# Extra edges in two lists of 64, one for each half of a pair, spread by products of 64 rows on two halves of the array

## What is computed

```python
summed = segment_sum(x[src], dst)
aggr = summed / max(count, 1)
h = aggr @ W_l.T + b_l + x @ W_r.T
h_norm = (h - mean(h)) * rsqrt(var(h) + 1e-5) * gamma + beta   # over the nodes
out = layernorm(x + relu(h_norm))                              # over the features
```

## Time and profile before

| | |
|---|---|
| median of 3 runs | 2502.92 us (2500.47 to 2504.99) |
| the profiled execution | 2496.8 us |
| its span, first to last instruction | 2495.1 us |
| mean granted TensorE clock | 0.853 |
| preparation and groups 0 to 7 | to about 172 us |
| loop over the pairs | first spread product 172.8 us, last 1736.2 us |
| second stage | behind about 1757 us |

### The profile page before, as it was taken

The page is one execution under the profiler, slowest core; times in us unless marked ns, Lnnn a source line. Parts: engine busy times, 40 slices in busy tenths (PEclk is TensorE's granted clock), DMA queues, the critical chain, the costliest instruction groups (busy, mean ns, idle before and its releaser), DMA issues. The chain is left out here.

```text
span 2495.1 us, 29831 instructions
## 1 busy us (share of the span) xinstructions
PE 1737.1 (70%) x9426; PEld 1411.9 (57%) x9426; DVE 1951.8 (78%) x3468; ACT 1471.2 (59%) x2847; POOL 1408.7 (56%) x688
## 2 busy tenths in 40 slices
PE   7999999999999999999999999998300000000000
PEld 5788888888888888888888888886100000000000
DVE  7846888888888888888888788887587777676666
ACT  4343555455554554555455545553499998888877
POOL 6034555555656655655556555556395655655654
PEclk9999999999999999999999999998755555555555
DMA  5567888878887888888888888888999999999998
GB/s 191 162 215 228 259 268 258 284 242 272 280 273 238 269 277 258 263 269 262 269 261 253 268 273 268 254 261 249 381 419 426 427 425 426 425 421 414 422 418 342
DMA packets 125536, 752.91 MB, mean 302 GB/s; under 512 B 20810, under 2 KB 20810, under 8 KB 65727
## 3 DMA queue, kind: packets, MB, share of 16 engines
q1 hardware_dynamic: 71710, 618.44, 65.9%
q0 software_dynamic: 53664, 132.51, 20.9%
HBM read 515.32 MB, written 246.22 MB: 305 GB/s over the span
## 5 line engine op out<-in xcount | busy, mean ns | idle before, releaser
L567 PE MATMUL pd<-wc_hi,x_hi 128*128 128x512 f32 x1564 | 626.7, 401 | 18.1 <-DVE wc_lo L970 15.3
L786 ACT ACTIVATE h_out<-pd 128x512 f32<-128x512 f32 x391 | 233.7, 598 | 656.8 <-PE pd L569 640.1
L569 PE MATMUL pd<-wc_hi,x_lo 128*128 128x512 f32 x1564 | 612.2, 391 | 0.0
L568 PE MATMUL pd<-wc_lo,x_hi 128*128 128x512 f32 x1564 | 609.3, 390 | 0.0
L1459 POOL TENSOR_TENSOR hx<-hx,scale_b 128x2560 f32<-128x2560 f32 (+2 forms) x99 | 441.3, 4478 | 286.1 <-DMA hx<-h_scratch 250.7
L1437 POOL DMA_INDIRECT h_scratch<-zz,si x156 | 324.2, 2078 | 412.1 <-ACT zz L832 192.9
L567 PEld LDWEIGHTS pd<-wc_hi,x_hi 128*128 128x128 f32 x1564 | 294.0, 188 | 75.5 <-issue 16.3
L930 ACT ACTIVATE hx<-hx,nr,rs 128x512 f32<-128x512 f32 x385 | 279.8, 802 | 89.0 <-DVE nr L1310 89.0
L569 PEld LDWEIGHTS pd<-wc_hi,x_lo 128*128 128x128 f32 x1564 | 293.7, 188 | 65.2
L568 PEld LDWEIGHTS pd<-wc_lo,x_hi 128*128 128x128 f32 x1564 | 294.6, 188 | 57.5
L1387 POOL DMA_INDIRECT xn<-x,gi x156 | 294.9, 1890 | 47.7 <-issue 44.3
(11 more groups left out here) (236 smaller groups left out, 3236.9 us busy)
## 6 DMA issues: line engine op xcount, KB each, us to landing
raw<-xT_whole SPq DMA_DIRECT2D x78, 1280.0 KB
h_scratch<-h_out SPq DMA_DIRECT2D x78, 1280.0 KB
hx<-x SPq DMA_DIRECT2D x78, 1280.0 KB, 20.6
hx<-h_scratch SPq DMA_DIRECT2D x77, 1280.0 KB, 15.4
out<-hx SPq DMA_DIRECT2D x77, 1280.0 KB, 18.1
hs<-h_scratch SPq DMA_DIRECT2D x76, 1280.0 KB
h_out<-h_scratch SPq DMA_DIRECT2D x2, 1280.0 KB, 7.3
xn<-x,gi POOLq DMA_INDIRECT x156
```

Source lines behind the costliest of these rows:

```text
L567: pe.matmul(pd[i][0:n, :], hi, wc["hi"][:, kc, :], start=kc == 0, stop=False)
L568: pe.matmul(pd[i][0:n, :], hi, wc["lo"][:, kc, :], start=False, stop=False)
L569: last = pe.matmul(pd[i][0:n, :], lo, wc["hi"][:, kc, :], start=False, stop=kc == KC - 1)
L786: act.activation(h_out[0:n, b, t, :], pd[(b + t) % 2][0:n, :], ACT.Copy).then_inc(s_ev, 1)
```

## The change

- The extras of half 0 are numbered 1 to 64 and those of half 1 from 65 to 128. For this DVE splits `member` by half (`b2["slot"]` for half 0, `vd` for half 1), sums those of half 0 over each window (`first_x`), and TensorE adds these over the partitions with one more bf16 product of 78 columns. DVE then subtracts this number from those of half 1 and adds 64. The bound for `left_over` is 64 for each half.
- The product of a half takes the 64 partitions of its list alone, so that there are four products with 64 rows, all ahead of the first plain tile, with the halves in turn. They increment `s_e` once, and the waits for it are changed to that.

```diff
+XH = P // 2
...
+        first_x = s0("first_x", [P, U], BF16)
...
-                last.then_inc(s_xrank, 1)
+                pe.matmul(p6[0:EB, 0:U], ones_b[0:EB, 0:EB], first_x[0:EB, :], start=True, stop=True).then_inc(s_xrank, 1)
...
-            def spread_extras(u, h):
-                if h == 0:
-                    pe.wait_ge(s_xel, u + 1)
-                    pe.wait_ge(s_spread, u + 1)
+            def spread_extras(u):
+
+                pe.wait_ge(s_xel, u + 1)
+                pe.wait_ge(s_spread, u + 1)
                 if u > 0:
-                    pe.wait_ge(s_d, 2 * u + h - 1)
-                to = spread[:, h * P:(h + 1) * P]
-                pe.matmul(spread_to[h][:], to, xe_hi[:], start=True, stop=False)
-                pe.matmul(spread_to[h][:], to, xe_lo[:], start=False, stop=True).then_inc(s_e, 1)
+                    pe.wait_ge(s_d, 2 * u)
+                for part in (xe_hi, xe_lo):
+                    for h in range(2):
+                        rows = slice(h * XH, (h + 1) * XH)
+                        last = pe.matmul(spread_to[h][:], spread[rows, h * P:(h + 1) * P], part[rows, :],
+                                         start=part is xe_hi, stop=part is xe_lo)
+                last.then_inc(s_e, 1)
...
                     if a is not None:
-                        spread_extras(a, 0)
+                        spread_extras(a)
                     plain(0)
-                    if a is not None:
-                        spread_extras(a, 1)
                     plain(1)
...
-                    act.wait_ge(s_e, 2 * u)
+                    act.wait_ge(s_e, u)
...
+            dve.scalar_tensor_tensor(vd, code, 1.0, vb, ALU.is_equal, ALU.mult)
+            dve.scalar_tensor_tensor(b2["slot"][a], code, 1.0, va, ALU.is_equal, ALU.mult)
             link(dve.tensor_tensor(va, va, vb, ALU.add))
             link(dve.scalar_tensor_tensor(b2["member"][a], code, 1.0, va, ALU.is_equal, ALU.mult))
+            with nc.allow_low_precision("whole numbers up to the number of blocks of a window"):
+                dve.tensor_reduce(first_x[a], b2["slot"][a].rearrange("p w u -> p u w"), AX.X, ALU.add)
...
-            dve.tensor_copy(xr[a].rearrange("p u w -> p w u"), vb)
+
+            link(dve.tensor_tensor(va, vd, p6[a, 0:U].unsqueeze(1).to_broadcast([EB, WIN, U]), ALU.mult))
+            link(dve.tensor_tensor(vb, vb, va, ALU.subtract))
+            dve.scalar_tensor_tensor(xr[a].rearrange("p u w -> p w u"), vd, float(XH), vb, ALU.mult, ALU.add)
             link(dve.tensor_reduce(cov[a, 1:2], vb, AX.XY, ALU.max))
-            link(dve.tensor_scalar(cov[a, 1:2], cov[a, 1:2], float(P), None, ALU.is_gt))
+            link(dve.tensor_scalar(cov[a, 1:2], cov[a, 1:2], float(XH), None, ALU.is_gt))
...
                 if u > 0:
-                    dve.wait_ge(s_e, 2 * u)
+                    dve.wait_ge(s_e, u)
...
             def difference(u, h):
-                dve.wait_ge(s_e, 2 * u + h + 1)
+                dve.wait_ge(s_e, u + 1)
```

## The result

The changed kernel takes 2506.43 us, the median of 12 runs (2502.76 to 2509.95), against 2500.34 us of the kernel before in the same comparison (2496.68 to 2506.80, 12 runs). The ratio is 1.0021, with a 95% interval of 1.0013 to 1.0028, so it is slower by 5.2 us (3.2 to 7.0). The ratio isn't that of the two medians, which lie 6.1 us apart; every difference to the kernel before is worked out here from such a ratio. The measured change lies at the bound of 0.2% that the prediction named. The profiled execution took 2504.56 us, its span is 2502.8 us, its mean clock 0.853.

A forecast was written before the change was run, and what follows sets the result against it. TensorE was taken to bound the loop over 78 pairs. Profiled 2496.8 us, plus 0 for the loop and 2 for the preparation, gave 2498.8; with 6.1 us to the runs' median, 2504.9, rounded 2505, range 2482 to 2539.

The forecast's parts named there:

- the bound of 0.2% that the prediction named: Whole kernel: a measurement can tell about 0.2%, 5 us, from no change.
- The mechanism of the loop: Spread group: side by side with both switches paid, 0.909 us a turn against 0.908; likeliest case, chance 0.50.
- one of the signs by which I said that I would be wrong: Preparation moving by more than 3 us; the other sign was the turn moving by more than 0.1 us.
- TensorE sets the loop: Loop over 78 pairs goes at TensorE's pace, 20.3 us a turn; a turn's cost or saving is the change's worth.
- Side by side: Spread group: two products on disjoint rows stream at once, so four take 0.454 us in place of 0.908.
- The way in and out, 0.20 us each, from `sum_cover`: Spread group: entering and leaving the smaller array each cost 0.09 + 0.11 = 0.20 us, read from `sum_cover`'s little products.
- The offset between the two of a pair: Spread group: the second product's load may wait for the first's, 0.00 to 0.11 us, taken as 0.055.
- What is moved: Half 1's products go ahead of the first tile; DVE's later difference is covered, costing nothing, up to 16 us otherwise.
- The preparation, +2 us: Before the loop: added DVE work delays TensorE by 1.3 to 2.9 us, taken as +2.
- The sum: Whole kernel: profiled 2496.8 + 0 + 2 = 2498.8 us, plus 6.1 us to the median of the runs: 2504.9.

The follow-up runs named there:

- same_rows: Changed kernel, but both halves take rows 0 to 63 of the spread and extras; ratio 1.0134 to the kernel before, 2537.5 us.
- stacked: Two lists of 64, each gathered twice, high parts over low parts, one full 128-row product a half, preparation hidden from TensorE; ratio 1.0199 to the kernel before.
- moved_only: Kernel before, with its four 128-row spread products all ahead of the first tile and one increment of `s_e`; ratio 1.0003.
- prep_only: Changed kernel's preparation with the kernel before's spread group of four 128-row products in their old places; ratio 1.0012 to the kernel before, 2504.65 us.
- spread_only: Kernel before's preparation with the changed kernel's spread group of 64-row products, some extras left out; ratio 0.9994 to the kernel before.
- half_by_half: Changed kernel with its products ordered half 0 high, half 0 low, half 1 high, half 1 low; ratio 1.0009 to the kernel before, 2504.9 us.
- before_again: The kernel before, unchanged, run for one more profile; 2501.8 us.
- no_waits: Changed kernel with the two-list work off DVE's path and the low parts of group 5 formed earlier; ratio 0.9982 to the kernel before, 2497.69 us.

## Why the prediction was right, and where not

The forecast was 2505 us, with a range of 2482 to 2539; 2506.4 was measured. That the two lie 1.4 us apart is in part luck. The forecast was built on 2502.9 us for the kernel before and a change of +2 us; in the comparison the kernel before took 2500.3, and the change was +5.2 (3.2 to 7.0). The mechanism of the loop was right. The term that was too small is the preparation, and one of the signs by which I said that I would be wrong, more than 3 us there, did come. Point by point:

- **TensorE sets the loop.** Right. same_rows adds 0.47 us to a regular turn, and its loop takes 1580.2 us, 31 more than the mean with the old group, which is 66 turns' worth; stacked's free turns are shorter by just its 0.45 us.
- **Side by side.** Right: both products of a pair start together, and same_rows shows that the disjoint rows are the reason.
- **The way in and out, 0.20 us each, from `sum_cover`.** Right to the hundredth: 0.32 us from the last product to the first load on both sides, and 0.11 us of load. This step carried the whole forecast. The rule of the Trainium skill ("TensorEngine Tiling (Array Packing)", "Key Properties"), that a change of mode drains TensorE, holds here, and its price eats the gain: 0.40 us against 0.454.
- **The offset between the two of a pair.** I took 0.055 us, the middle of 0.00 and 0.11. It is 0.00 (0.01 at most, and 0.03 where the group begins with a wait); loads for different rows run at once. The group takes 0.86 us. A regular turn, though, gains only 0.013 us and not 0.05: behind the uncovered load the next six products or so step at up to 0.237 us, not 0.227, which gives 0.03 us back. The same small loss stands behind the transposes of each turn before. I had left it out.
- **The way in where TensorE waits.** In every tenth turn TensorE stands idle for `xe_lo` just ahead of the group, with the old group and with the new one alike. Here are the first spread product and the second plain product, in moved_only (four full products) and then in the changed kernel:

```profile
581.57 0.47 PE L659 MATMUL pe<-xe_hi,spread 128*128 128x512 f32 x1 [0.59 <-DVE xe_lo L1132]
...
582.80 0.39 PE L570 MATMUL pd<-wc_lo,x_hi 128*128 128x512 f32 x1
```

```profile
582.16 0.46 PE L661 MATMUL pe<-xe_hi,spread 64*128 64x512 f32 x1 [0.58 <-DVE xe_lo L1141]
...
583.16 0.40 PE L571 MATMUL pd<-wc_lo,x_hi 128*128 128x512 f32 x1
```

From the one to the other are 1.23 us with full products and 1.00 us with small ones. The smaller products gain 0.23 us here, because the way in lies inside a wait that is there anyway. That is seven times 0.22 us beyond what regular turns gain, 1.5 us. With 0.013 us for each of 77 turns, 1.0 us, the loop should give back some 2.5 us, inside my -4 to +4. The means of the loops show 0.2 us; the rest is in the irregular turns.
- **What is moved: nothing.** Right, by moved_only.
- **The preparation, +2 us.** This term was mis-sized. In the profile it is +3.9 us; over the profiles with the old preparation and its old order (172.8, 174.1, 173.5, 175.9 us to the first spread product) and with the new (176.8, 178.9, 178.8, 176.5, 178.5) the means are 174.1 and 177.9, so 3.8 us. Without what the clock did it is 3.3 us: up to the start of group 7 the two old profiles whose clock stays at 1.00 take 130.3 and 130.7 us, the three new ones that lose nothing to the clock 133.8, 133.6 and 133.9. Two things failed. The strided write took 3.70 us, 1.7 more than the copy, where I had given 0 to 0.5: I took the price of the strided copy (one input) for an operation with two, though the forms without a stride differ too, 0.56 and 0.97 us. And the trace of the kernel before held a nearer row, two operations of the same form, with two inputs and a bf16 output with another stride, 2.80 and 2.96 us:

```profile
75.34 5.47 DVE L1047 SCALAR_TENSOR_TENSOR vals<-got,e_d 125x780 bf16<-125x780 f32 x2
```

The second thing: I counted a wait of TensorE at its length alone. Behind the new wait of 1.8 us the clock fell in 2 of the 5 profiles that have it, for 1.4 and 1.5 us.
- **The sum.** Preparation +3.8 and loop -0.2, both as means over the profiles, give +3.6 us, which lies within the 3.2 to 7.0 us measured for the changed kernel. With the 2.5 us that the steps of the loop should give back it would be +1.3 us, and prep_only and spread_only together give +1.5 us, with some 2 us to each side of either. So 1.6 us of the 5.2 are missing by the first sum, and nearly 4 by the other two; the intervals are wide enough to take up most of either. Irregular turns behind late transfers are where the profiles show such time; whether the change makes them stays open.

## What to carry to other kernels

Two small products on disjoint rows do stream at once, but going into the smaller form and out of it costs 0.40 us and some 0.03 us behind it. Against 0.227 us gained by a pair of 512 columns, two pairs a visit come out even, which is what was measured; more than two should pay (an estimate from these numbers, no run had more). It also pays where TensorE waits ahead of the group anyway: there two pairs gained 0.23 us. Look for the one place in the old trace where the form already changes: it gave that price to the hundredth before anything was built. In a stage that one engine fills, extra work in a preparation isn't free because it is done once: ask what it makes that engine wait for, price each operation by a row with as many inputs and the same kind of output, and put it behind what the engine needs first.

## What the runs showed of the hardware that I had not expected

- TensorE started products out of program order when their rows were disjoint: the third started with the first, 0.33 us ahead of the second (half_by_half).
- A wait of 1.8 to 2.8 us may be followed by products at 1.2 GHz, steps of 0.43 us in place of 0.227, or may not, in executions of the same code: 2.8 us lost in moved_only, 1.4 us in before_again, nothing in the first profile of before. So part of the spread between executions can be that; no_waits, which has no such wait, doesn't show a smaller one.
- Behind a load that nothing covered, some six products stepped at up to 0.237 us in place of 0.227, 0.03 us in all.
- A DVE operation with two inputs and a strided bf16 output over 780 elements took 3.70 us, two with another stride 2.80 and 2.96 us (L1047 of the kernel before), one with one input and the stride of the first 1.97 us, and one with two inputs and a plain output 0.97 us.
